# A four-layer graph network on one core: small arrays loaded between the first stores, and the messages of layers 1 to 3 multiplied in two pieces

## The reference

```
layer 0   msg = relu([x[src], x[dst], edge] @ W1 + b1);  agg = mean of msg by dst (W2 after it)
          x + relu([x, agg] @ U1 + c1) @ U2 + c2, layernorm with gamma, beta
layers 1 to 3 (attention, 4 or 8 heads)
          e     = leaky_relu(a_src[src] + a_dst[dst])            per edge and head
          p     = exp(e - max of e over the edges of a target)
          msg   = h[src] * p   per head;   out = sum of msg by dst / sum of p by dst
          (layer 1: plus skip product and layernorm; layer 3: batch norm, relu, residual)
```

## Time and profile before

| what | value |
|---|---|
| median of 3 runs | 12334.37 us (12312.73 to 12349.45) |
| the profiled execution: time, span | 12336.85 us, 12335.1 us |
| busy: PE, PEld | 7368.8 us (60%), 6500.9 us (53%) |
| busy: DVE, ACT, POOL | 5183.6 us (42%), 2180.5 us (18%), 6252.3 us (51%) |
| mean granted TensorE clock | 0.727 of full speed |
| gathers (L568) | 6448, 6112.1 us busy, 948 ns each |
| chain that ended last | 29% put down to another core or an unknown queue, PE 25%, DVE 23%, issue 16% |

### The profile page before, as it was taken

The page is one execution under the profiler, slowest core; times in us unless marked ns, Lnnn a source line. Parts: engine busy times, 40 slices in busy tenths (PEclk is TensorE's granted clock), DMA queues, the critical chain, the costliest instruction groups (busy, mean ns, idle before and its releaser), DMA issues.

```text
span 12335.1 us, 141293 instructions
## 1 busy us (share of the span) xinstructions
PE 7368.8 (60%) x41611; PEld 6500.9 (53%) x41612; DVE 5183.6 (42%) x13628; ACT 2180.5 (18%) x7255; POOL 6252.3 (51%) x6594
## 2 busy tenths in 40 slices
PE   5666666666565555665565555555555555565554
PEld 5655555555555545554455555554544555555554
DVE  3222222224444444444464444444445444444445
ACT  2111111112111111111121111111112111111112
POOL 4555555554455545554445555555544555555553
PEclk7777777777777777777767777777776777777776
DMA  3222222222211111111122121121112221111111
GB/s 88 55 55 55 55 54 55 56 55 59 51 47 47 47 45 47 47 46 45 46 67 48 47 48 48 48 48 48 47 47 55 49 48 48 48 48 48 48 48 42
DMA packets 425594, 625.69 MB, mean 51 GB/s; under 512 B 189754, under 2 KB 305737, under 8 KB 425285
## 3 DMA queue, kind: packets, MB, share of 16 engines
q0 software_dynamic: 206336, 462.61, 15.4%
q1 hardware_dynamic: 218910, 160.84, 5.0%
q10 hardware_dynamic: 296, 1.65, 0.0%
HBM read 598.03 MB, written 26.58 MB: 51 GB/s over the span
## 4 chain that ended last, share of the span: by engine, by line
another core or an unknown queue 29%; PE 25%; DVE 23%; issue 16%; DVEq 4%; ACT 2%; POOL 1%; DMA 0%; SPq 0%; ACTq 0%; POOLq 0%
PE ps L713 12%; PE ps L760 7%; DVE acc L1263 5%; DVE memb L1183 4%; DVEq L1237 2%; PE ps L703 2%; DVE msg L1356 2%; DVE msg L1276 1%; DVEq L1263 1%; PE ps L791 1%; DVE acc L1253 1%; DVE shared L1310 1%; PE ps L795 1%; DVE shared L1348 1%
## 5 line engine op out<-in xcount | busy, mean ns | idle before, releaser
L568 POOL DMA_INDIRECT G<-rows,idx x6448 | 6112.1, 948 | 5686.5 <-DVE msg L1356 2881.2
L713 PE MATMUL ps<-msg,memb 128*128 128x136 f32 (+2 forms) x12896 | 2052.4, 328 | 62.9 <-DVE msg L1356 62.2
L760 PE MATMUL ps<-membT,shared 128*104 128x128 f32 x9672 | 2082.8, 400 | 2.2 <-ACT membT L925 2.2
L713 PEld LDWEIGHTS ps<-msg,memb 128*128 128x128 f32 x12896 | 1976.0, 236 | 84.0 <-issue 41.1
L760 PEld LDWEIGHTS ps<-membT,shared 128*104 128x104 f32 x9672 | 1874.9, 270 | 29.5 <-issue 3.0
L703 PE MATMUL ps<-ident,memb 128*128 128x128 f32 x6448 | 1108.2, 302 | 1137.5 <-issue 750.3
L1183 DVE TENSOR_TENSOR memb<-rel,ps 128x768 f32<-128x768 f32 x1488 | 1044.4, 729 | 1509.1 <-PE ps L713 1227.7
L703 PEld LDWEIGHTS ps<-ident,memb 128*128 128x128 f32 x6448 | 770.4, 150 | 1393.4 <-issue 1034.4
L925 ACT ACTIVATE membT<-ps 128x512 f32<-128x512 f32 x1984 | 991.3, 510 | 1961.8 <-remote 1639.2
L732 PE MATMUL ps<-shared,membT 128*128 x3224 | 813.8, 336 | 754.2 <-DVE msg L1276 472.5
L1263 DVE TENSOR_TENSOR acc<-acc,ps 128x136 f32 (+2 forms) x3472 | 1023.0, 295 | 561.7 <-issue 315.5
(11 more groups left out here) (182 smaller groups left out, 4864.9 us busy)
## 6 DMA issues: line engine op xcount, KB each, us to landing
G<-rows,idx POOLq DMA_INDIRECT x6448
shared<-marks_all SPq DMA_DIRECT2D x372, 156.0 KB
shared<-in_edge_attr SPq DMA_DIRECT2D x124, 256.0 KB
shared<-in_edge_attr SPq DMA_DIRECT2D x124, 160.0 KB
rows<-msg SPq DMA_DIRECT2D x36, 288.0 KB, 2.7
idx<-in_src SPq DMA_DIRECT2D x496, 6.5 KB
xrows<-msg SPq DMA_DIRECT2D x24, 256.0 KB, 2.2
memb<-xrows SPq DMA_DIRECT2D x24, 256.0 KB, 2.9
```

The source lines that it names most:

```text
L568: nc.gpsimd.indirect_dma_start(G[:, b, t, 0:rows[l].shape[1]], None, rows[l], bass.IndirectOffsetOnAxis(idx[:, b, t:t + 1], 0)).then_inc(g ...
L713: last = mm(ps_sum[k // 2][:, 0:width], memb[:, b, k * P:(k + 1) * P], msg[:, b, k, 0:width], start=k % 2 == 0, stop=k % 2 == 1 or k == K - 1)
L760: last = mm(ps_sc[b][0:JH, :], adz[:, k // 2, K - 1 - k:K - 1 - k + JH], membT[:, k, :], start=k == 0, stop=False)
```

## The change

Two things are edited.

**The messages.** In layers 1 to 3, L1356 becomes two instructions, over tiles 0 to 5 (`FIRST` = 6) and 6 to 12. The first raises a new semaphore, `first_messages`, the second `messages`. TensorE waits for the first ahead of its sums and for the second ahead of tile 6; GpSimd waits for the first ahead of the gather of tile 0 and for the second ahead of that of tile 6, in layer 0 too, where VectorE's sequencer raises both one after the other.

**The set-up.** The 13 columns, the 6 spread vectors and the 5 turned weights are laid side by side in one array each before the launch, so that 35 loads become 13. All 13 are issued between the stores of the first table's blocks; the edge features of chunk 0 come behind store 3, those of chunk 1 last.

```diff
+            store_first(0)
             for h in range(2):
                 load(w1e[h * ED:(h + 1) * ED, h, :], A["L0_gnn_W1"][2 * P:2 * P + ED, :])
+            store_first(1)
+            load(cols[:, :], A["vector_cols"])
+            store_first(2)
+            load(scratch[:, SO:SO + 5 * P], A["turned_weights"])
+            store_first(3)
+            load_edge_features(0, 0)
+            store_first(4)
+            load(u1[:, :, :], A["L0_gnn_U1"].rearrange("(h p) n -> p h n", p=P))
+            store_first(5)
+            load(reps[:, :, :].rearrange("p k n -> p (k n)"),
+                 A["vector_rows"].rearrange("(o n) -> o n", o=1).to_broadcast([P, len(REP) * P]))
...
+            store_first(10)
+            load(wsk[:, :], A["L1_gnn_skip_W"])
+            for s in range(11, NS):
+                store_first(s)
+            load_edge_features(1, 1)
@@ edges, GpSimd
                 if not early:
-                    pool.wait_ge(messages, past(l, c - 2))
+                    pool.wait_ge(first_messages, past(l, c - 2))
                 pool.sem_inc(gather_paced, 1)
                 for t in range(K):
+                    if t == FIRST and not early:
+                        pool.wait_ge(messages, past(l, c - 2))
+                        pool.sem_inc(gather_paced, 1)
                     nc.gpsimd.indirect_dma_start(
@@ sums and attention, TensorE
+                    if l and k == FIRST:
+                        pe.wait_ge(messages, past(l, c))
...
-                pe.wait_ge(messages, past(l, c))
+                pe.wait_ge(first_messages, past(l, c))
@@ mlp, VectorE
                 dve.wait_ge(pre_added[3], past(0, c))
+                dve.sem_inc(first_messages, 1)
                 dve.sem_inc(messages, 1)
@@ attention, VectorE
-                tt(msg[:, b, :, 0:MW].rearrange("p k (h f) -> p k h f", h=H),
-                   G[:, b, :, 0:MW].rearrange("p k (h f) -> p k h f", h=H),
-                   ps_wgt.rearrange("p (h k) -> p k h", h=H).unsqueeze(3).to_broadcast([P, K, H, FW]),
-                   ALU.mult).then_inc(messages, 1)
+                for k0, k1, done_with in ((0, FIRST, first_messages), (FIRST, K, messages)):
+                    tt(msg[:, b, k0:k1, 0:MW].rearrange("p k (h f) -> p k h f", h=H),
+                       G[:, b, k0:k1, 0:MW].rearrange("p k (h f) -> p k h f", h=H),
+                       ps_wgt.rearrange("p (h k) -> p k h", h=H)[:, k0:k1, :].unsqueeze(3)
+                       .to_broadcast([P, k1 - k0, H, FW]), ALU.mult).then_inc(done_with, 1)
```

More of the change, by code:

```diff
@@ L3 @@
 from contextlib import ExitStack
+VECTOR_COLS = ["L0_gnn_c1", "L0_gnn_b2", "L3_gnn_bias", "L3_gnn_gamma", "L3_gnn_beta", "L1_gnn_att_src",
+               "L1_gnn_att_dst", "L2_gnn_attn_l", "L2_gnn_attn_r", "L3_gnn_att_src", "L3_gnn_att_dst",
+               "L2_gnn_b_src", "L2_gnn_b_dst"]
+VECTOR_ROWS = ["L0_gnn_gamma", "L1_gnn_ln_g", "L0_gnn_c2", "L1_gnn_gat_bias", "L0_gnn_beta", "L1_gnn_ln_b"]
+TURNED = ["L1_gnn_W", "L2_gnn_W_src", "L2_gnn_W_dst", "L3_gnn_W", "L0_gnn_W2"]
 def gnn_program(nc, A, out):
@@ L181, in gnn_program @@
         b2_u1 = sb("b2_u1", [1, P])
-        COL = {n: k for k, n in enumerate(
-            ["L0_gnn_c1", "L0_gnn_b2", "L3_gnn_bias", "L3_gnn_gamma", "L3_gnn_beta", "L1_gnn_att_src",
-             "L1_gnn_att_dst", "L2_gnn_attn_l", "L2_gnn_attn_r", "L3_gnn_att_src", "L3_gnn_att_dst",
-             "L2_gnn_b_src", "L2_gnn_b_dst"])}
-        REP = ["L0_gnn_gamma", "L1_gnn_ln_g", "L0_gnn_c2", "L1_gnn_gat_bias", "L0_gnn_beta", "L1_gnn_ln_b"]
+        COL = {n: k for k, n in enumerate(VECTOR_COLS)}
+        REP = VECTOR_ROWS
         cols = sb("cols", [P, len(COL)])
@@ L1687 @@
     arrays["x_cols"] = np.ascontiguousarray(_lay(a["x"], -n % 512, 0).T)
[L1688 to L1689 removed]
+    arrays["turned_weights"] = np.ascontiguousarray(np.concatenate([a[name].T for name in TURNED], axis=1))
+    arrays["vector_cols"] = np.ascontiguousarray(np.stack([arrays[name] for name in VECTOR_COLS], axis=1))
+    arrays["vector_rows"] = np.ascontiguousarray(np.concatenate([arrays[name] for name in VECTOR_ROWS]))
+    for name in ["L0_gnn_W2", "L2_gnn_W_src", "L2_gnn_W_dst"] + VECTOR_COLS + VECTOR_ROWS:
         del arrays[name]
[L1691 to L1692 removed]
     arrays["src"] = np.ascontiguousarray(_lay(a["src"], pad, 0).reshape(chunks, K, P).transpose(0, 2, 1))
```

28 lines of the change are left out of this document (8 added, 20 removed).

## The result

| | before | after |
|---|---|---|
| median of 4 runs each, same chip | 12337.31 us (12312.73 to 12349.45) | 12590.44 us (12587.30 to 12594.29) |
| ratio, 95% interval | | 1.0208 (1.019 to 1.0226) |
| profiled execution: time, span | 12336.85, 12335.1 us | 12594.29, 12592.5 us |
| mean granted TensorE clock | 0.727 | 0.696 |

The change makes the kernel 2.1% slower; 12,234 us was forecast. In the new file the messages' multiplication is L1376, the gathers L584, the scan of tile ends L1329, what waits for the carries (L1337 before) L1356, the sums L731.

What follows compares the result with a forecast made beforehand. Bound taken: a ring of multiplication, 13 gathers, TensorE's output 2.50 us after them, and the chain from L1337. Terms -91 + 0 - 10 = -101 us against 12336.85 gave 12,236, median forecast 12,234; range 12,000 to 12,430.

Steps and rivals of the forecast that it cites:

- the first gather at T+1.79: GpSimd, T being the start of multiplication L1356: first gather forecast 1.8 us behind T instead of 2.78, 0.99 us earlier.
- the added wait: GpSimd's second wait, ahead of the seventh gather: taken as 0, at the dear end 234 us; drained-queue rival 12,467, chance 0.03.
- the usual chunk: Layers 1 to 3, from one multiplication's start to the next: 23.76 us before, L1337 starting at T+21.23; forecast to gain 0.99.
- long chunks take over: Rival: TensorE late between sums and L772; 45% and 30% of chunks turn, at 1.51 or 4.33 us each; 12,434, chance 0.20.
- The usual chunk holds, with 1.7 to 3.0 to spare, and gains 0.99: Layers 1 to 3: L1310, needed by T+17.67, comes at T+14.6 to T+15.9, so the chunk shortens by 0.99 us.
- the lag worked out from rows 2, 3 and 4: From three profiled chunks: gathers 0.99 us earlier make L1310 start 1.9 to 3.2 us later against T.
- 25% of the chunks of layers 2 and 3 as turning long: Share assumed to lose 1.51 us while the rest gain 0.99: -0.37 us a chunk, -91 us over 248 chunks.
- layer 1 at break-even: Layer 1's loop: gains and long chunks assumed to cancel, at 19% turning long; term 0 us.
- A short chunk: Layers 1 to 3: chunk with L1310 at T+9.76 and next T at T+21.45; not excepted from the 0.99 us gain.
- 2.5 us after the last of them has been issued: What TensorE owes, for which L1337 waits, comes 2.5 us after the last gather's issue; release forecast at T+20.24.
- -10 us forecast: Set-up: earlier loads start the 27th gather 12 us earlier, less 2 us for later stores; ends -20 and +5.
- the release is TensorE's own: Rival: TensorE late for a reason gathers don't share; L1337 stays at T+21.2, only set-up moves; 12,324, chance 0.14.

Runs made afterwards that it cites:

- e1: Kernel before with the whole message change (multiplication in two, split waits on GpSimd and TensorE), old set-up; second chip: 1.0031 of before.
- e3: Kernel before with two multiplications; TensorE waits for each piece, GpSimd for the second alone, old set-up; second chip: 0.9833 of before.
- e4: Kernel before with two multiplications; GpSimd waits for first then second, TensorE for both ahead of its sums, old set-up; second chip: 1.0168 of before.
- e16: The form of e3 against the kernel before, on the first kind of chip: 12,296 us against 12,337, ratio 0.9962.
- e13: Kernel before, but in layers 1 to 3 gathers of tiles 7 to 12 fetch 16 rows instead of 128, except each layer's first two chunks: 12,318 us against 12,337.
- e18: Kernel before with an unused 128 x 512 memset on GpSimd between seventh and eighth gather of each chunk of layers 1 to 3: 12,297 us, as before.
- e9: The changed kernel itself, unedited, on another chip of the first kind, against the kernel before: 1.0192.
- e2: Kernel before with the new set-up alone (35 loads become 13, all between the stores), second chip: 0.9969 of before.
- e17: Kernel before, but in layers 1 to 3 GpSimd issues only the gathers of tiles 0 to 6, except each layer's first two chunks: 9,910 us.

## Why the prediction was wrong

**What held.** The steps that say where things move: pieces of 1.00 and 1.14 us (1.01 and 1.15 forecast); the first gather at T+1.79, no longer gap ahead of the seventh (all gaps between the gathers of a chunk are 0.30), so the added wait is free, and layer 0's chunk, 23.46 us, became 23.50; L1337's release at T+20.2; the usual chunk some 0.9 to 1.0 us shorter; VectorE's extra instruction hidden. The rival "long chunks take over" names the place rightly. It has the price nearly right in layers 2 and 3 (long chunks take 25.6 and 25.4 us, 1.6 to 1.8 over 23.76, against 1.51) and too high in layer 1 (26.8, 3.0 over it, against 4.33, which came from the single chunk of the earlier trace rows). The time passed even its 12,434.

**The step that failed** is "The usual chunk holds, with 1.7 to 3.0 to spare, and gains 0.99". The chunk that it was worked out for the earlier trace rows begins with TensorE at half clock and its sums at T+2.68. Of such chunks, by the table above, 186 of 222 are long in the changed kernel and only 37 of 270 were before. Their L1310 stands at T+20.11 in the median, where T+14.6 to T+15.9 was forecast and T+14.87 was the median before. So the lag worked out from rows 2, 3 and 4, 1.9 to 3.2 us, was too small for them: their median moved by 5.2 us (their mean by 3.4). The mean over all chunks moved by 2.4, 2.2 and 1.9 us (layers 1 to 3) and so lies at or inside the forecast, but that is luck: it mixes chunks at T+20 with chunks near full clock at T+12, of which there are 144 and were 96.

With that step fell the terms of the sum. It took 25% of the chunks of layers 2 and 3 as turning long and had layer 1 at break-even, at 0. Long are 42% and 45%, and 69% in layer 1, whose loss is 154 of 257 us.

**Would a count have helped?** The 25% was taken from the means, and counting was possible: in the trace of before L1310 stands above T+15 in 50, 45 and 51 of 122 chunks. But 19, 11 and 7 of these are long already, so that 31, 34 and 44 were left to turn: 25%, 28% and 36%. With the prediction's own gain and prices that gives about 0 for the three layers in place of -91 us. It is still no loss of 250. Nor are they the chunks that turned: 125 of the 190 long chunks of after stood at T+15 or below before. Whether a chunk is long goes with the one before it (127 of 173 behind a usual one, 60 of 190 behind a long one) and with the clock that it begins at. That the clock is the link is read from these counts; no run held it fixed. That the earlier gathers are the cause of the loss is shown by e1, e3, e4 and, on the first kind, by e16.

**A smaller term missing.** A short chunk can't gain 0.99: with 22.0 us it was below the new usual 22.8 already. Of the 52, 30 turned long, and the others take 22.9.

**The release.** The reading "2.5 us after the last of them has been issued" was a coincidence of 13 gathers; e13 and e18 refute it, and it holds in number only. The forecast of the new T+20.2 survives because both move with the first gather.

**Set-up.** -10 us forecast, within -20 to +5; +9 measured. The stores took 8.6 us more, not the 2 taken; three loads of `wext` among them held SyncE's queue for 12.7 us. The other half, that earlier loads bring TensorE's products forward, failed in the changed kernel and in e9, where they came 41.1 and 40.6 us behind the first gather as before (40.5), and held in e2 on the second chip, at 15.1. So it is no rule either way, and what decides it stays open.

**The rivals.** That the release is TensorE's own falls (e17). The rule that the prediction weighed from the Trainium skill (Runtime: NRT & Kernel Launch, section "Instruction fetch mechanics"), a stall at a taken branch out of the fetched window, falls with it: e17 has the same loop and branches, and its release comes 8.4 us earlier. That a delay by the instruction looks like instructions that arrive late is an argument; no run here shows what is fetched when.

## What to carry to other kernels

Where the time of a repeated stage has several values, count them from the trace before a mean is believed, and ask what each leaves to the next: here long and usual chunks take turns, and a share worked out chunk by chunk misses that. When two engines wait for one semaphore, splitting it is two changes: give the earlier release to the one that then works and keep it from the one whose work disturbs the other (here, on chips with a late TensorE, the sums and not the gathers: 0.9962 instead of 1.0208). Before transfers are moved ahead of others in one queue, read how long each holds it (12.7 us for three here). And measure the kernel before beside each experiment, on the same chip.

## What the runs showed of the hardware

- The same kernel took 8,768 us on one chip, 12,297 to 12,339 on three and in the first measurement, and 13,048 on one. With GpSimd's gathers at 946 to 951 ns each on all of them, the difference is TensorE's output being late while indirect gathers are under way: not at all, or until 18.44 or some 18.7 us behind the first of 13.
- Where it is late, it is so from 5 us behind the first gather, until 18.44 with 13 of them and 10.04 with 7: 1.40 us for each gather more, and as long with 16 rows in six of the 13 as with 128. Two more products of TensorE cost 1.1 us a chunk (416 us / 372), 1 x 1 or 128 x 128.
- A wait in the middle of GpSimd's queue that is met when it comes costs nothing: 0.30 us between the gathers, with it and without.
- TensorE idle for 5.4 us began the next chunk at half clock; ten matmuls took 2.43 us instead of 1.26, and the 26 of the sums 4.03 instead of 3.28.
- The three loads of `wext` held SyncE's queue for 6.1 us behind the 13 stores and for 12.7 us among them.
